# Gated scan and expert layer on one core: the last addition of the output rows as an accumulating DMA, and work at other places

## The chip, the core and the metric

The program runs on one core of a Trainium2 chip. The metric is the device time of one execution in microseconds (us): 694.19 is the median of three runs of the kernel before, which lie between 693.59 and 695.44.

## What is computed

The input x is 8 batches of 1024 tokens of 256 numbers. Two layers follow each other, each with a layer norm ahead of it, one behind it and a residual. The first mixes, for each token, the two best of four gated linear recurrences over the tokens:

```python
gate_logits = einsum('bsd,dm->bsm', x, gate_W)
top_vals, top_idx = top_k(gate_logits, 2);  weights = softmax(top_vals)
g, v, d = (x @ W[m] + b[m] for each mixer m)          # Wg, Wv, Wd
a = 0.001 + 0.998 * sigmoid(d)
h = linear_scan(sigmoid(g) * tanh(v), a)              # h_t = a_t h_{t-1} + x_t
return sum over m of comb[..., m] * h[m]              # comb: weights at top_idx, else 0
```

The second sends each batch row to one of eight experts, by the mean of its normed tokens:

```python
z = layernorm(x) * ln_g + ln_b;  z_bn = batchnorm(mean(z, tokens))
probs = softmax(z_bn @ Wr + br);  idx = argmax(probs);  gate = probs[idx]
h = relu(z @ W_down[idx] + b_down[idx])               # 256 -> 64
return (h @ W_up[idx] + b_up[idx]) * gate             # 64 -> 256
```

Around them: x = x + layernorm(mix(layernorm(x))), then x = x + layernorm(experts(layernorm(x))).

## The kernel before

Each engine has its program written out by hand; the order of its lines is the order of its work, and semaphores tie the engines together. Every engine's program has three parts: `run_first` for batch 0, `run` for batches 1 to 6, which a loop of three turns with two batches each repeats (`iterations`, L230), and `last` for batch 7. In these, `bt` is the batch whose recurrences are computed, `nx` the next one, whose x is loaded, normed, split in two 16-bit halves (`xh`, `xl`) and weighed for the mixers, and `pv` the previous one, whose second layer is done between the products of `bt`.

A batch's recurrences are 8 planes (4 mixers by 2 halves of 128 channels). For each plane TensorE makes 6 products of 128 channels by 512 tokens (gate, decay and value, for two chunks of tokens), 48 in a batch, numbered i=0 to 47. A product is six 16-bit matmuls (L1332) into one of three banks of `ps_main`; ScalarE evacuates each with its sigmoid or tanh (`evacuate`, L550 to L580, into `gate_s`, `decay_s` and `hid`), and TensorE waits for the bank that it wants next. VectorE multiplies (L902), scans (L884) and weighs each plane with `comb_all` (`weigh`, L896), the token weights, which come broadcast through DRAM. GpSimd's accumulating DMAs add up planes of `hid` (`add_plane`, L477). In `last` the batch is cut in two halves of 512 tokens, so that the tail can start on the first.

What is done for `pv` hangs on numbers i in the programs of TensorE (`run`, L1441) and ScalarE (L677), which say ahead of which product or evacuation a step stands. TensorE turns the added planes into token rows (`turn_planes`, L1346); VectorE takes their moments (`a_moments`, L784), adds the residual into `resid`, takes moments again; ScalarE norms (`normalise_t`, L616, into `normed`); TensorE turns the result (`turn_u`), ScalarE copies it to `u_split` (`high_u`, L587); VectorE and TensorE (`route`) make the router's logits, VectorE picks the index (`route_pick`, L942), SyncE reads it and loads that expert's weights (`load_expert`, L328). Then TensorE's `down` (L1382), ScalarE's `hidden_part` and `high_h`, VectorE's `join_h` and `low_h` (L964), TensorE's `up` (L1391), moments and shift, and ScalarE's `scale_rows` (L639), which leaves the normed expert rows in `normed`, or in `x_in` under the name `late_rows` for batches 6 and 7. `normed` also carries x's halves on their way to `xh` and `xl`. GpSimd makes the roots of the variances (`power`, L464).

At a batch's end VectorE's `finish` (L987) adds `normed` to `resid`; for batches 6 and 7 `finish_late` (L994) does it tile by tile. SyncE's `store` (L340) then writes `resid` out at the end of its turn in `run`, after the next x, this batch's x for `resid` (`load_resid`, L335), the expert, x's moved halves (`move_x`) and `comb_all` (`load_weights`, L314).

## Time and profile before

| | |
|---|---|
| median of three runs | 694.19 us (693.59 to 695.44) |
| the profiled execution | 692.3 us |
| its span, first to last instruction | 690.5 us |
| TensorE (PE) busy | 610.8 us, 88% |
| VectorE (DVE) busy | 586.9 us, 85% |
| ScalarE (ACT) busy | 460.5 us, 67% |
| GpSimd (POOL) busy | 100.9 us, 15% |
| granted TensorE clock, mean | 0.958 of full |

The span has a start up to some 31 us, batch 0 up to about 100 us, six batches of the loop with 76.5 us each (177.0 to 253.5 is the second of them), and the last batch with its tail from about 560 us. Busy shares are means over these stages. In the loop TensorE's matmuls follow each other nearly without a break, and what counts there is what it waits for; behind 643 us the engines work one after another and the chain of waits is what counts. Matmuls are pipelined: one is drawn with 0.38 us, but the next starts 0.22 us after it. PEld is TensorE's loading of weights, SPq the queue of DMAs that SyncE issues.

### The profile page before, as it was taken

To read this page: it belongs to the slowest core of one execution; us is meant where nothing else is said; L and a number is where in the kernel's file an instruction comes from. 1 tells how busy PE (TensorE), PEld (TensorE's weight loads), DVE (VectorE), ACT (ScalarE), POOL (GpSimd) and SP (SyncE) were. 2 spreads that over 40 slices of the span, in tenths; PEclk is the share of its full clock that TensorE was granted. 3 is DMA by queue.
4 is the path that set the end of the run, shared out by engine and by line. 5 is a ranking of instruction groups with operands and counts; after the bars stand their busy time and mean duration, and the time that the engine had idled before them with its cause. 6 is when DMAs were issued, how large, how long until landed. Compare 5 with 4: busy or idle time off the path is not lost. (4 is left out here: it accounts for less than half of the span.)

```text
span 690.5 us, 10277 instructions
## 1 busy us (share of the span) xinstructions
PE 610.8 (88%) x3259; PEld 312.7 (45%) x3259; DVE 586.9 (85%) x1096; ACT 460.5 (67%) x789; POOL 100.9 (15%) x103
## 2 busy tenths in 40 slices
PE   3799999899999999899999999899999997989432
PEld 1345454445544554445544554444544554444321
DVE  6699688998889888998889888998889888778846
ACT  3657555896579666986589666987589667657213
POOL 2002012101121102101121102101121101112101
PEclk9999999999999999999999999999999999999655
DMA  8652636162533617171724626161816433301121
GB/s 227 142 183 39 146 63 243 20 130 47 204 103 75 120 59 251 31 133 33 233 73 92 103 79 227 42 122 31 271 33 116 79 122 124 59 14 32 31 72 61
DMA packets 74905, 73.63 MB, mean 107 GB/s; under 512 B 36166, under 2 KB 66154, under 8 KB 74858
## 3 DMA queue, kind: packets, MB, share of 16 engines
q1 hardware_dynamic: 69676, 56.30, 28.8%
q0 software_dynamic: 5184, 16.78, 13.3%
q8 instruction: 22, 0.36, 0.2%
q14 instruction: 23, 0.19, 0.1%
HBM read 38.85 MB, written 8.52 MB: 69 GB/s over the span
## 5 line engine op out<-in xcount | busy, mean ns | idle before, releaser
L1332 PE MATMUL ps_main<-xh,w_hi 128*128 128x512 f16 x768 | 293.9, 383 | 16.0 <-ACT gate_s L574 9.3
L1332 PE MATMUL ps_main<-xh,w_lo 128*128 128x512 f16 x768 | 293.5, 382 | 0.0
L1332 PE MATMUL ps_main<-xl,w_hi 128*128 128x512 f16 x768 | 293.3, 382 | 0.0
L884 DVE TENSOR_TENSOR_SCAN hid<-decay_s,hid 128x1024 f32<-128x1024 f32 (+1 forms) x64 | 138.2, 2159 | 6.6
L574 ACT ACTIVATE decay_s<-ps_main,vecs 128x512 f32<-128x512 f32 x128 | 88.1, 688 | 72.9 <-PE ps_main L1332 72.1
L574 ACT ACTIVATE hid<-ps_main,vecs 128x512 f32<-128x512 f32 x128 | 88.3, 690 | 62.3 <-PE ps_main L1332 61.9
L1332 PEld LDWEIGHTS ps_main<-xh,w_hi 128*128 128x128 f16 x768 | 76.4, 99 | 110.1 <-ACT gate_s L574 16.1
L1332 PEld LDWEIGHTS ps_main<-xl,w_hi 128*128 128x128 f16 x768 | 75.7, 99 | 92.4 <-issue 3.0
L1332 PEld LDWEIGHTS ps_main<-xh,w_lo 128*128 128x128 f16 x768 | 75.7, 99 | 85.0 <-issue 2.3
L574 ACT ACTIVATE gate_s<-ps_main,vecs 128x512 f32<-128x512 f32 x128 | 87.7, 685 | 29.9 <-PE ps_main L1332 28.8
L896 DVE TENSOR_TENSOR hid<-hid,comb_all 128x1024 f32<-128x1024 f32 (+1 forms) x72 | 79.6, 1106 | 2.5
L902 DVE TENSOR_TENSOR hid<-gate_s,hid 128x1024 f32<-128x1024 f32 (+1 forms) x72 | 79.4, 1103 | 1.4 <-ACT hid L574 0.5
L580 ACT ACTIVATE decay_s<-decay_s 128x1024 f32<-128x1024 f32 (+1 forms) x72 | 69.0, 959 | 0.0
L477 POOL DMA_DIRECT2D hid<-hid x36 | 31.8, 882 | 246.5 <-DVE hid L896 238.4
L1283 PE MATMUL ps_aux<-ident,normed 128*128 128x128 f32 x144 | 22.3, 317 | 33.8 <-DVE normed L824 20.5
L464 POOL TENSOR_TENSOR root_a<-root_in_a,neg_half 128x8 f32<-128x8 f32 (+1 forms) x9 | 19.3, 2142 | 136.7 <-DVE root_in_a L792 136.7
L1283 PEld LDWEIGHTS ps_aux<-ident,normed 128*128 128x128 f32 x144 | 19.3, 164 | 38.4 <-ACT normed L616 17.3
L1346 PE MATMUL ps_aux<-ident,hid 128*128 128x128 f32 x256 | 31.2, 280 | 3.0 <-DMA hid<-hid 2.6
L1346 PEld LDWEIGHTS ps_aux<-ident,hid 128*128 128x128 f32 x256 | 29.5, 145 | 5.7 <-issue 3.4
L784 DVE BATCH_NORM_STATS2 stats_a<-ps_aux 128x6 f32<-128x256 f32 x64 | 22.1, 416 | 11.6 <-PE ps_aux L1346 11.6
L616 ACT ACTIVATE normed<-resid,shift_t,root_t 128x256 f32<-128x256 f32 x60 | 30.4, 592 | 2.2 <-DVE shift_t L799 2.2
L784 DVE BATCH_NORM_STATS2 stats_y<-ps_aux 128x6 f32<-128x256 f32 x64 | 22.1, 417 | 11.4 <-PE ps_aux L1392 11.4
(139 smaller groups left out, 581.3 us busy)
## 6 DMA issues: line engine op xcount, KB each, us to landing
comb_all<-comb_dram SPq DMA_DIRECT2D x32, 512.0 KB, 5.5
hid<-hid POOLq DMA_DIRECT2D x28, 512.0 KB, 4.6
x_in<-in_L_attn_x SPq DMA_DIRECT2D x16, 512.0 KB, 10.0
resid<-in_L_attn_x SPq DMA_DIRECT2D x8, 1024.0 KB, 5.9
out<-resid SPq DMA_DIRECT2D x7, 1024.0 KB, 9.9
hid<-hid POOLq DMA_DIRECT2D x8, 256.0 KB, 3.3
expert<-experts SPq DMA_DIRECT2D x8, 192.5 KB, 2.2
w_stage<-in_L_attn_Wg SPq DMA_DIRECT2D x4, 256.0 KB, 3.5
```

The costliest lines, as they stand in the source:

```text
L464: pool.tensor_tensor(root[key][:, span(c)], root_in[key][:, span(c)], neg_half[:, span(c)], ALU.pow).then_inc(rooted, units(c))
L477: pool.dma_start(hid[:, p + KT, tokens(c)], hid[:, p, tokens(c)], accum_op=ALU.add).then_inc(plane_added[p], 16)
L574: act.activation(dst, ps_main[:, i % BANKS], ACT.Tanh if kind == VALUE else ACT.Sigmoid, bias=vecs[:, col:col + 1], scale=Q_W).then_inc(ma ...
L580: act.activation(d, d, ACT.Copy, bias=0.001, scale=0.998).then_inc(decay_ready, 1)
L616: ins = act.activation(out[:, t], rows[:, t], ACT.Identity, bias=shift[key][:, t:t + 1], scale=root[key][:, t:t + 1])
L784: ins = dve.bn_stats(out=stats[key][:, t], in_=rows(t))
L884: dve.tensor_tensor_scan(states(pc), staged(decay_s, pc, pc.c), states(pc), start, ALU.mult, ALU.add).then_inc(scanned, 1)
L896: dve.tensor_tensor(src, src, comb_all[:, m, tokens(pc.c)], ALU.mult).then_inc(weighed, 1)
L902: dve.tensor_tensor(v, staged(gate_s, pc, pc.c), v, ALU.mult).then_inc(input_ready, 1)
L1283: ins = pe.transpose(ps_aux[:, KT * cc + k, tile(t % (T // C))], normed[:, t, k * P:(k + 1) * P], ident[:])
L1332: ins = pe.matmul(ps_main[:, i % BANKS], w[:, 3 * m + kind, k, half * P:(half + 1) * P], v[:, bt.par, span(c), k], start=(n == 0), stop=(n ...
L1346: ins = pe.matmul(ps_tok[:, t, k * P:(k + 1) * P], hid[:, p, tile(t)], ident[:], is_transpose=True, start=(p == TURNED[0] and t % 2 == 0), ...
```

## The change

- `finish` and VectorE's addition for batches 0 to 6 are gone. GpSimd's `add_rows` waits until ScalarE's normed expert rows are written (`y_normed`) and issues one DMA that adds 1 MB of `normed` (for batch 6 `late_rows`) to `resid`; `rows_added` tells when it has landed. In `run` it is GpSimd's last step; in `last` it stands behind the roots of t.
- `store` waits for `rows_added` and stands one turn later: in `run` straight behind the load of the next x and ahead of `load_resid`. SyncE's program has no loop any more; its eight turns are written out. In `last` the store of batch 5 comes first, and that of batch 6 stands ahead of `load_expert(bt)`.
- ScalarE waits for `rows_added` before it overwrites `normed` (`normalise_t`) and `late_rows`.
- In `run` TensorE turns the planes at i=3 (was 4), does `down` at 30 (29), `up` at 38 (40), the next batch's gates at 41 (40). ScalarE makes both halves of u at i=20 (were 20 and 21), `high_h` at 33 and 35 (31 and 34), `shares` at 47 (44), the first rows at 44 (45). VectorE's `x_moments`, `scale_x` and `weights_of` stand a plane or a part of one later.
- In batch 0 VectorE's preparations of the weights are in another order, TensorE makes the first gates and turns the weights at i=4 (6 and 8), the next gates at 38 (36). In the last batch `up` is at i=32 (29), and at the end VectorE makes the moments of both halves before the shifts.

The diff, cut to its core, by engines. SyncE and GpSimd:

```diff
@@ -336,7 +337,7 @@
                              ).then_inc(resid_loaded, 16)
 
             def store(pv):
-                sp.wait_ge(out_ready, done(pv))
+                sp.wait_ge(rows_added, 16 * pv.n + 16)
                 sp.dma_start(out_t[bass.ds(pv.n, 1)].rearrange("a p t d -> p (a t) d"), resid[:, pv.par]
                              ).then_inc(out_stored, 16)
 
@@ -417,26 +418,32 @@
                 load_resid(bt)
                 load_weights(bt, nx)
 
-            def run(bt, nx, pv):
+            def run(bt, nx, pv, before):
                 load_next_x(bt, nx)
+                if before:
+                    store(before)
                 load_resid(bt)
                 load_expert(pv)
                 move_x(nx)
                 load_weights(bt, nx)
-                store(pv)
-
-            def last(bt, pv):
+
+            def last(bt, pv, before):
+                store(before)
                 load_resid(bt)
                 load_expert(pv)
+                store(pv)
                 load_expert(bt)
-                store(pv)
                 for part in range(2 * C):
-                    sp.wait_ge(out_ready, C * bt.n + part + 1)
+                    sp.wait_ge(out_ready, part + 1)
                     s = slice(part * T // (2 * C), (part + 1) * T // (2 * C))
                     sp.dma_start(out_t[bt.n, :, s], t_rows(bt)[:, s]).then_inc(out_stored, 16)
                 sp.wait_ge(out_stored, 16 * (B + 2 * C) + 1)
 
-            iterations(sp, run_first, run, last)
+            turns = [Batch(n, n % 2, n == B - 1) for n in range(B)]
+            run_first(turns[0], turns[1])
+            for n in range(1, B - 1):
+                run(turns[n], turns[n + 1], turns[n - 1], turns[n - 2] if n > 1 else None)
+            last(turns[B - 1], turns[B - 2], turns[B - 3])
 
 
         @block.gpsimd
@@ -477,6 +484,12 @@
                 pool.dma_start(hid[:, p + KT, tokens(c)], hid[:, p, tokens(c)], accum_op=ALU.add
                                ).then_inc(plane_added[p], 16)
 
+            def add_rows(pv, rows):
+
+                pool.wait_ge(y_normed, T * (pv.n + 1) + 1)
+                pool.sem_inc(rows_go, 1)
+                pool.dma_start(resid[:, pv.par], rows[:], accum_op=ALU.add).then_inc(rows_added, 16)
+
...
                 add_plane(bt, 3)
                 power("y", y_root_in, y_root, pv)
+                add_rows(pv, normed)
...
                 power("t", t_root_in, t_root, bt, 1)
+                add_rows(pv, late_rows)
                 power("y", y_root_in, y_root, bt, 0)
                 power("y", y_root_in, y_root, bt, 1)
```

ScalarE, the waits and `run`:

```diff
             def normalise_t(pv, ts):
 
                 act.wait_ge(t_scaled, done(pv))
+                act.wait_ge(rows_added, 16 * pv.n)
                 normalise("t", t_rows(pv), ts, u_ready, C if ts[-1] == T - 1 else 0)
...
             def scale_late_rows(bt, c):
                 act.wait_ge(y_scaled, B + c)
+                act.wait_ge(rows_added, 16 * (B - 1))
                 scale_rows(bt, tiles(c), late_rows)
...
                         normalise_t(pv, tiles(1))
                     if i == 20:
                         high_u(pv, 0)
-                    if i == 21:
                         high_u(pv, 1)
                     if i == 24:
...
                         hidden_part(pv, 1)
-                    if i == 31:
+                    if i == 33:
                         high_h(pv, 0)
-                    if i == 34:
+                    if i == 35:
                         high_h(pv, 1)
                     if i == 44:
-                        shares(nx)
-                    if i == 45:
                         act.wait_ge(xh_moved, 16 * nx.n)
                         act.wait_ge(xl_moved, 16 * nx.n)
                         act.wait_ge(y_scaled, pv.n + 1)
                         scale_rows(pv, (0, 1, 2), normed)
+                    if i == 47:
+                        shares(nx)
                     evacuate(bt, i, bank, False)
```

VectorE: `finish` and `finish_late`, the start of `run_first`, the end of `last`:

```diff
-            def finish(pv):
-
-                dve.wait_ge(y_normed, T * (pv.n + 1) + 1)
-                rows = t_rows(pv)
-                dve.tensor_tensor(rows, normed[:], rows, ALU.add).then_inc(out_ready, C)
-
             def finish_late(b, c):
 
                 rows = t_rows(b)
                 for t in tiles(c):
                     dve.wait_ge(y_normed, T * b.n + t + 2)
                     ins = dve.tensor_tensor(rows[:, t], late_rows[:, t], rows[:, t], ALU.add)
-                    if b.cut and t % 2:
+                    if t % 2:
                         ins.then_inc(out_ready, 1)
-                if not b.cut:
-                    ins.then_inc(out_ready, C)
...
             def run_first(bt, nx):
                 prep = linker(prep_link, 0)
                 pcs = pieces(bt)
+                prepare_router(prep)
                 mixer_low(1)
                 prepare_down(prep, 0)
-                set_ones()
                 rank_mixers(bt)
                 weights_of(bt)
-                mixer_low(2)
+                set_ones()
+                prepare_down(prep, 1)
                 copy_weights(bt, True)
-                mixer_low(3)
-                prepare_router(prep)
-                prepare_down(prep, 1)
                 prepare_up_biases(prep)
...
                 weigh(bt, pcs[15])
+                low_u(bt, 0)
                 a_moments(bt, 1)
-                low_u(bt, 0)
                 residual(bt, 1)
                 t_moments(bt, 1)
                 scale_t(bt, 1)
                 normalise("t", t_rows(bt), t_scaled, u_ready, bt, 1)
                 route_logits(bt)
-                finish_late(pv, None)
+                route_pick(bt)
                 low_u(bt, 1)
                 join_h(bt, 0)
-                route_pick(bt)
                 join_h(bt, 1)
                 low_h(bt, 0)
                 low_h(bt, 1)
                 y_moments(bt, 0)
+                y_moments(bt, 1)
                 scale_y(bt, 0)
-                y_moments(bt, 1)
+                scale_y(bt, 1)
                 finish_late(bt, 0)
-                scale_y(bt, 1)
                 finish_late(bt, 1)
```

TensorE: `run_first`, `run` and `last`:

```diff
                 for i, bank in enumerate(banks(bt)):
                     if i == 0:
                         turn_vecs()
-                    if i == 2:
                         turn_x(bt, 1)
-                    if i == 6:
+                    if i == 4:
                         first_gates(bt)
-                    if i == 8:
                         turn_weights(bt)
-                    if i == 21:
+                    if i == 20:
                         hidden_bias()
-                    if i == 36:
+                    if i == 38:
                         pe.wait_ge(experts_ready, 6)
                         gates(nx)
                     product(bt, i, bank, True)
...
             def run(bt, nx, pv):
                 for i, bank in enumerate(banks(bt)):
-                    if i == 4:
+                    if i == 3:
                         turn_planes(pv, (4, 5, 6, 7))
                     if i == 22:
                         turn_u(pv)
                     if i == 26:
                         route(pv)
-                    if i == 29:
+                    if i == 30:
                         down(pv)
-                    if i == 40:
+                    if i == 38:
                         up(pv)
+                    if i == 41:
                         gates(nx)
...
                         turn_u(pv)
-                    if i == 16:
+                    if i == 17:
                         route(pv)
-                    if i == 23:
+                    if i == 24:
                         down(pv)
-                    if i == 29:
+                    if i == 32:
                         up(pv)
-                    if i == 39:
+                    if i == 38:
                         pe.wait_ge(y_normed, T * (B - 2) + T // C + 1)
                         turn_planes(bt, TURNED, 0)
-                    if i == 47:
-                        turn_u(bt, 0)
                     product(bt, i, bank, False)
+                turn_u(bt, 0)
                 pe.wait_ge(y_normed, T * (B - 1) + 1)
                 turn_planes(bt, TURNED, 1)
```

The order of the instructions on SyncE at the program's end shows where the store of batch 6 stands against the two loads of an expert's weights. Before (`load_resid`, `load_expert` for batches 6 and 7, the store, the four parts of batch 7):

```order
L335 DMA resid<-in_L_attn_x 128x8x256
L327 TENSOR_LOAD index
L327 ISA x2
L328 ISA
L328 DMA expert<-experts 128x385
L327 TENSOR_LOAD index
L327 ISA x2
L328 ISA
L328 DMA expert<-experts 128x385
L340 DMA out<-resid 128x8x256
L436 DMA out<-resid 128x2x256 x4
```

After, with the same steps:

```order
L336 DMA resid<-in_L_attn_x 128x8x256
L328 TENSOR_LOAD index
L328 ISA x2
L329 ISA
L329 DMA expert<-experts 128x385
L341 DMA out<-resid 128x8x256
L328 TENSOR_LOAD index
L328 ISA x2
L329 ISA
L329 DMA expert<-experts 128x385
L439 DMA out<-resid 128x2x256 x4
```

The store, the first DMA into `out`, was behind both loads of `expert` and now stands between them.

On ScalarE around i=19 to 21 in the loop, `normed` x8 is `normalise_t`, `u_split` are `high_u`'s copies, and `gate_s`, `decay_s` and `hid` are evacuations. Before:

```order
L574 ACTIVATE decay_s<-ps_main,vecs 128x512
L586 ISA
L587 ACTIVATE u_split,u_sums<-ps_aux 128x512
L586 REGISTER_ALU
L587 ACTIVATE u_split,u_sums<-ps_aux 128x512
L573 REGISTER_ALU
L574 ACTIVATE hid<-ps_main,vecs 128x512
L586 REGISTER_ALU
L587 ACTIVATE u_split,u_sums<-ps_aux 128x512
L586 REGISTER_ALU
L587 ACTIVATE u_split,u_sums<-ps_aux 128x512
```

After:

```order
L589 ACTIVATE decay_s<-ps_main,vecs 128x512
L601 ISA
L602 ACTIVATE u_split,u_sums<-ps_aux 128x512
L601 REGISTER_ALU
L602 ACTIVATE u_split,u_sums<-ps_aux 128x512
L601 REGISTER_ALU
L602 ACTIVATE u_split,u_sums<-ps_aux 128x512
L601 REGISTER_ALU
L602 ACTIVATE u_split,u_sums<-ps_aux 128x512
L588 REGISTER_ALU
L589 ACTIVATE hid<-ps_main,vecs 128x512
```

All four copies of u now stand ahead of the evacuation into `hid` (i=20), where two of them came behind it.

On GpSimd at the program's end the rows are the additions of planes (`hid`), the roots of a, t and y, and in the new program the addition into `resid`. Before:

```order
L477 DMA hid<-hid 128x512
L464 TENSOR_TENSOR root_t<-root_in_t,neg_half 128x4
L477 DMA hid<-hid 128x512 x2
L464 TENSOR_TENSOR root_a<-root_in_a,neg_half 128x4
L464 TENSOR_TENSOR root_t<-root_in_t,neg_half 128x4
L464 TENSOR_TENSOR root_y<-root_in_y,neg_half 128x4 x2
```

After:

```order
L484 DMA hid<-hid 128x512
L471 TENSOR_TENSOR root_t<-root_in_t,neg_half 128x4
L484 DMA hid<-hid 128x512 x2
L471 TENSOR_TENSOR root_a<-root_in_a,neg_half 128x4
L471 TENSOR_TENSOR root_t<-root_in_t,neg_half 128x4
L491 DMA resid<-x_in 128x2048
L471 TENSOR_TENSOR root_y<-root_in_y,neg_half 128x4 x2
```

The addition for batch 6 comes behind the last roots of a and t and ahead of those of y.

## Rows read from the trace of the kernel before

**Rows 1.** Windows table, a loop batch: busy us (x instructions) per engine, clock, DMA, GB/s
```profile
177.00:253.50 76.50, 72.72 (x400) 36.92 (x398) 68.62 (x122) 56.84 (x97) 11.84 (x8) 1.00 0.44 114
```

**Rows 2.** Waits of TensorE, whole span: waiter <- releaser: us, times, longest
```profile
PE ps_main L1332 <- ACT gate_s L574: 9.3, 10, 1.2
PE ps_aux L1391 <- DVE up_in L964: 5.7, 2, 2.9
...
PE ps_aux L1382 <- DMA expert<-experts: 3.1, 6, 0.8
...
PE ps_misc L1303 <- DMA xl<-normed: 1.3, 1, 1.3
```

**Rows 3.** Timeline of TensorE: start us, duration us, what, [idle before <-releaser]
```profile
31.46 0.39 PE L1332 MATMUL ps_main<-xh,w_hi 128*128 128x512 f16 x1 [3.66 <-ACT decay_s L574]
...
175.55 0.39 PE L1332 MATMUL ps_main<-xh,w_hi 128*128 128x512 f16 x1 [0.58 <-ACT gate_s L574]
...
213.73 0.38 PE L1332 MATMUL ps_main<-xl,w_hi 128*128 128x512 f16 x1
215.22 0.39 PE L1332 MATMUL ps_main<-xh,w_hi 128*128 128x512 f16 x1 [1.10 <-ACT gate_s L574]
215.44 0.38 PE L1332 MATMUL ps_main<-xh,w_lo 128*128 128x512 f16 x1
...
218.45 1.90 PE L1382 MATMUL ps_aux<-u_split,expert 128*128 128x512 f16 x8 [0.47 <-DMA expert<-experts]
```

**Rows 4.** Timeline of ScalarE, second batch of the loop
```profile
207.28 0.60 ACT L587 ACTIVATE u_split<-ps_aux 128x512 f16<-128x512 f32 x1
...
214.28 0.21 ACT L592 ACTIVATE r<-r 128x8 f32<-128x8 f32 x1 [1.10 <-DVE r L938]
```

**Rows 5.** Timeline of VectorE, same batch
```profile
176.72 2.27 DVE L987 TENSOR_TENSOR resid<-normed,resid 128x2048 f32<-128x2048 f32 x1
180.55 2.75 DVE L784 BATCH_NORM_STATS2 stats_a<-ps_aux 128x6 f32<-128x256 f32 x8 [1.55 <-PE ps_aux L1346]
...
187.82 1.22 DVE L896 TENSOR_TENSOR hid<-hid,comb_all 128x1024 f32<-128x1024 f32 x1
```

**Rows 6.** The page's DMA issues: queue, count, KB each, median us to landing
```profile
comb_all<-comb_dram SPq DMA_DIRECT2D x32, 512.0 KB, 5.5
hid<-hid POOLq DMA_DIRECT2D x28, 512.0 KB, 4.6
x_in<-in_L_attn_x SPq DMA_DIRECT2D x16, 512.0 KB, 10.0
...
out<-resid SPq DMA_DIRECT2D x7, 1024.0 KB, 9.9
hid<-hid POOLq DMA_DIRECT2D x8, 256.0 KB, 3.3
expert<-experts SPq DMA_DIRECT2D x8, 192.5 KB, 2.2
```

**Rows 7.** SyncE's queue, timeline; last, the DMA issues after 600 us
```profile
178.34 2.58 SPq L314 DMA_DIRECT2D comb_all<-comb_dram  x4
...
667.00 0.49 SPq L328 DMA_DIRECT2D expert<-experts  x1
...
out<-resid SPq DMA_DIRECT2D x1, 1024.0 KB, 4.5
```

**Rows 8.** The chain of work that ended last: start us, us, what
```profile
657.72 1.02 POOL root_t L464
...
666.10 0.05 DVE index L942
...
666.17 2.76 DVE resid L994 x8
...
670.28 1.88 PE ps_aux L1382 x4
```

**Rows 9.** Timeline of ScalarE at the end
```profile
685.49 1.93 ACT L639 ACTIVATE x_in<-ps_aux,shift_y,root_y 128x256 f32<-128x256 f32 x4 [1.82 <-DVE shift_y L980]
```

69 lines of the change are left out of this document (30 added, 39 removed).

## The prediction

> **What bounds the kernel now.** I read the windows table first. In a batch of the loop TensorE shows 72.7 us of 76.5 and VectorE 68.6 [rows 1]; what is left of TensorE's time are short stalls, and a gain in the loop must come out of them. The waits of TensorE name them [rows 2], and its timeline places them [rows 3]. Three kinds recur, and I call the 48 products of a batch i=0 to 47. First, ten waits on ScalarE's evacuation of `gate_s`, 9.3 us: four of 0.58 at i=3 (the row at 175.55; batches 2, 4, 5, 6), the other six, some 1.1 each, at i=27 (the row at 215.22). Second, `down` waits for the expert's weights in each of six batches, 3.1 us together. Third, outside the steady part, 1.3 us for the moved halves of x in batch 0, and `up` in the last batch. A matmul starts 0.22 after its predecessor but is drawn 0.38 long [rows 3], so a stall costs 0.17 more in starts than its idle: 215.22 lies 1.49 after 213.73, 1.27 too late. Behind the loop the chain of waits reads as one thread, with VectorE's eight additions of the previous rows, 2.76 us, standing in it [rows 8].
>
> **The change, part by part.** All prices are against the profiled execution, 692.3 us (span 690.5 and 1.8 around it), which is 1.9 under the median of 694.2 of the runs shown; I add that at the end.
>
> *VectorE's addition goes in the loop.* Six instructions of 2.27 [rows 5] leave VectorE, 13.6 us busy. I price that at 0: straight behind it VectorE sat 1.55 us waiting for TensorE's turned planes [rows 5], so it would only wait longer. What it is worth must show through the next edit.
>
> *The planes are turned at i=3, not 4* (D). The four stalls at i=3 come since ScalarE first scales five tiles and then evacuates bank 0. With the turning there, TensorE has work just when it would stand still: 4 x (0.58 + 0.17) = **-3.0**. The bound on the other side is 0, if the planes' own inputs aren't there yet.
>
> *VectorE's lead and the router* (C). The turned planes come one product, 6 x 0.22 = 1.3 us, earlier in TensorE's order, and with them the chain to the router's logits. ScalarE stood 1.10 us for these logits before evacuating bank 24 [rows 4], and that is what TensorE waits for at i=27. Not all comes back: the logits also need TensorE's `route`, which isn't earlier, so about half, 0.8 of the 1.3 in starts at best. Against it, ScalarE now makes both halves of u at i=20 in a row: bank 20 is evacuated two copies, 1.1 us [rows 4], later. TensorE has turned u in the meantime and has a product of 1.3 in hand, so I take 0.3 of that. Net -0.5, six times: **-3.0**. Bounds: -6.6 if the 1.10 goes whole, +2.1 if VectorE gains no lead and 0.35 a batch is lost.
>
> *`down` one product later* (B). `down` waited 0.47 in the row at 218.45, 0.5 on the mean [rows 2, 3]; a product of 1.3 ahead of it covers that: 6 x (0.52 + 0.17) = **-4.1**, bound 0.
>
> *New waits* (F). The sigmoid of the shares moves from i=44 to 47, just ahead of the product of `comb` and `share` that TensorE turns at the batch's end, and `high_h` moves from 31 and 34 to 33 and 35, closer to `up`, which itself moves from 40 to 38. Each has less than a product of room. No row shows such a wait; the bounds are 0 and the largest wait of this sort, 1.2 a place [rows 2], of which 0.2 in each of six batches is nearest to the 0 that these edges show now: **+1.2**, range 0 to 2.4.
>
> *The addition as a DMA, in the loop.* It runs from `normed` on GpSimd's queue at the batch's end. Accumulating 256 KB takes 3.3 us and 512 KB 4.6 [rows 6], so 1 MB some 7.2. Who waits: ScalarE at i=19 before it overwrites `normed`, over 20 us later; SyncE's store, which now stands behind the loads of x; behind it the load of `resid`, which is used a batch later, and the expert's, 30 us on. GpSimd's next instruction, the root of a, comes only after the planes. Price 0; the cover is those distances. The store itself moves only from the end of one turn past the two loads of the next. Writing SyncE's turns out: 0, its queue waits for data nearly all the time.
>
> The Trainium skill (DMA: Bandwidth & Descriptors, Anatomy of one DMA — SWDGE (gpsimd) path) prices a transfer on this path at 2.0 us plus bytes over 436 GB/s, an estimate of 3.2 us for the 512 KB. The rows show 4.6, so the trace disagrees, and I leave it at that; by the page 1 MB would need 4.4 and the end (E, below) would come up to 2.8 us sooner.
>
> *Batch 0* (A). Gates of the next batch move from i=36 to 38, past the 1.3 us wait: -1.5. Against it, the first weights are turned at i=4 straight behind the gates. TensorE now stands idle 3.66 before i=7 [rows 3]; there it will stand with three products, 3.9 us, fewer done, while the ranking, with fewer copies ahead of it on VectorE, ends some 2.7 sooner: +1.2. **-0.3**, bounds -1.5 and +2.5.
>
> *Last batch and end* (E). `up` moves from i=29 to 32, so three products fill a wait of up to 2.9 [rows 2]; VectorE, which goes on from there without pause, gets perhaps 1.1 of it: -1.1. Then the chain: the 2.76 of additions leave VectorE's path between the index and `down`. What is late next is the expert's load. It was asked for at 667.00, 0.8 after the index, and takes 2.2 [rows 6, 7], so 669.2 would allow `down` at 669.3 and not 670.28. But SyncE now first waits for the addition to store batch 6. GpSimd asks for that after the root of t, which ends at 658.74 [rows 8]: with 0.5 for the issue it lands at 658.7 + 0.5 + 7.2 = 666.4, the store takes 4.5 [rows 7], 670.9, and the expert's load stands behind it in the same queue; x, asked for straight behind a store, takes 10.0 beside the store's 9.9 [rows 6]. With 0.5 for its own bytes, 671.4: +1.1 against 670.28. At the end VectorE makes both halves' moments before the first shift; ScalarE's gap of 1.82 [rows 9] closes while its first tiles start some 1.0 later: -0.8. Together **-0.8**, bounds -3.9 (the expert not held up) and +2.0 (the addition takes twice 4.6).
>
> **Sum:** -3.0 - 3.0 - 4.1 + 1.2 - 0.3 - 0.8 = -10.0; 692.3 - 10.0 = 682.3, and with 1.9 for the median 684.2.
>
> **The rivals.** *1. VectorE's lead is eaten* before the logits, by a later load or since ScalarE itself is full between i=19 and 33. For it: ScalarE waits only for VectorE there, and the recovered time must pass through it. Against: three banks of buffer. C is +2.1 instead of -3.0: 684.2 + 5.1 = 689.3.
>
> *2. Slower: the addition delays `comb_all`.* The 1 MB starts just before the four loads of `comb_all`, on the same 16 DMA engines. VectorE wants the first at 187.82; it was asked for at 178.34 and takes 5.5 [rows 5 to 7]: 4.0 to spare, 2.7 with a lead of 1.3. If the load gets nothing until the addition is done, it is up to 7.2 late: VectorE stands 4.5, hence 3.2 behind its old place, and ScalarE and TensorE wait that much more at i=27: C becomes 6 x 3.2 = +19.2, and 684.2 + 22.2 = 706.4. The kernel ends slower than 694.2 once C is over +7.0, 1.2 a batch, which is a delay of 2.7 + 1.3 + 1.2 = 5.2. Against it: the delay must be most of the addition's length, though the loads are asked for after the addition has begun.
>
> The Trainium skill (DMA: Bandwidth & Descriptors, Queues, rings and completion order) says an engine takes turns between queues packet by packet; by that the load would lose about half of the time, 3.6 us, and rival 2 would not come about. No run here shows the two side by side.
>
> *3. The change doesn't reach the steady part:* ScalarE, not TensorE, paces i=19 to 33, B and C both vanish: 684.2 + 7.1 = 691.3, hardly told from no change. For it: each of these waits lies where ScalarE runs without pause; against it: after i=33 ScalarE waits for TensorE again, so time that TensorE saves there is kept.
>
> **How the numbers follow.** Forecast 0.56; rival 1 0.20; rival 3 0.14; rival 2 0.10. A measurement tells 0.3%, 2.1 us, from no change: faster is under 692.1. The forecast and rival 1 are, and a third of rival 3 with its spread: 0.80; same 0.11; slower 0.09. The range leaves out rival 2 and the far half of rival 3: from 680.0 (C and E a little better) to 691.5.
>
> **What would show it.** In the new trace: no additions of 2.27 on VectorE; i=3 without a wait before it; ScalarE's wait for the logits under 0.7, not 1.1; `down` without a wait for the expert in the loop, and with one at the end, where the store is asked for before the expert; the 1 MB landing after 7 us. I am wrong if a batch stays at 76 us, if VectorE waits for `comb_all`, or if batch 0 ends later by more than 2.

## The result, and the profile after

The changed kernel takes 699.89 us (median of four runs, 698.94 to 700.43), the kernel before beside it 693.89: a ratio of 1.0093 with a 95% interval of 1.0051 to 1.0135. It is slower by 0.9%, where 1.4% faster was forecast. Its profiled execution took 700.2 us with a span of 698.0, against 692.3 and 690.5.

From the page of the changed kernel, span, and busy time of each engine:

```profile
span 698.0 us, 10188 instructions
...
PE 618.4 (89%) x3259; PEld 312.5 (45%) x3259; DVE 571.4 (82%) x1082; ACT 460.8 (66%) x789; POOL 100.8 (14%) x110
```

VectorE is busy 15.5 us less, as it should be without the additions of seven batches (13.6 and 2.8 us, [rows 5, 8]). TensorE, ScalarE and GpSimd have the work that they had; TensorE's drawn time grows by 7.6. The two traces, cut where the first product (i=0) of each batch starts, tell where the 7.5 us of span come from:

| us | start | batch 0 | 1 | 2 | 3 | 4 | 5 | 6 | 7 and tail |
|---|---|---|---|---|---|---|---|---|---|
| before | 14.2 | 80.0 | 76.7 | 77.9 | 75.9 | 76.5 | 76.7 | 76.5 | 136.1 |
| after | 16.6 | 80.5 | 75.7 | 79.9 | 77.3 | 79.6 | 77.4 | 76.1 | 135.0 |
| difference | +2.4 | +0.4 | -1.0 | +2.0 | +1.4 | +3.1 | +0.7 | -0.4 | -1.1 |

A batch that no turn of the loop touches (1 and 6) is shorter, as forecast, though by 0.4 to 1.0 and not by some 1.5. Batches 2 to 5 are longer, by 7.2 together, and the loop's two turns back lie at the ends of batches 2 and 4. The waits of TensorE after (what waits and releaser; us in total, times, longest) show the same place, beside [rows 2]:

```profile
PE ps_main L1327 <- issue: 7.4, 2, 3.8
PE ps_aux L1377 <- DMA expert<-experts: 5.6, 1, 5.6
...
PE ps_main L1327 <- ACT gate_s L589: 3.6, 7, 0.9
PE ps_aux L1386 <- DVE up_in L969: 3.5, 2, 2.9
...
PE ps_main L1327 <- ACT hid L589: 2.9, 6, 0.5
```

The ten waits on `gate_s`, 9.3 us, are seven of 3.6 now, and the expert's weights are waited for once, at the end, and no more in the loop. New are two waits of 3.7 on the mean with "issue" behind them: TensorE waited there for nothing that a semaphore shows. TensorE's timeline at the first turn, after:

```profile
248.31 0.38 PE L1327 MATMUL ps_main<-xl,w_hi 128*128 128x512 f16 x1
248.58 0.28 PE L1306 MATMUL ps_misc<-ident,comb 128*32 128x128 f32 x1
252.66 0.60 PE L1327 MATMUL ps_main<-xh,w_hi 128*128 128x512 f16 x1 [3.80 <-issue]
253.05 0.63 PE L1327 MATMUL ps_main<-xh,w_lo 128*128 128x512 f16 x1
```

L1306 turns `comb`, the next batch's token weights, the last work of a batch; the next row is the first product of batch 3. Between their starts lie 4.08 us. In the kernel before, they lie 1.43 apart at this turn and 0.11 at the second (3.86 after):

```profile
247.34 0.27 PE L1311 MATMUL ps_misc<-ident,comb 128*32 128x128 f32 x1
248.77 0.39 PE L1332 MATMUL ps_main<-xh,w_hi 128*128 128x512 f16 x1 [1.16 <-ACT hid L574]
```

What TensorE does in between stands in the view of one line, the loop's own: its three branches in the changed kernel, shortest, middle and longest in ns, then the first and last start (the shortest is the last, which falls through; PEldq stands for TensorE's sequencer, which issues its work):

```profile
L237 PEldq COMPARE_BRANCH  x3: 83/3400/3617, 248.7 to 562.8; - x3
```

and the same for the kernel before:

```profile
L236 PEldq COMPARE_BRANCH  x3: 76/236/3772, 244.6 to 551.5; - x3
```

TensorE's branch back to the loop's head is drawn 3.4 to 3.8 us long in both programs, but for one of 0.24 in the kernel before. The kernel before starts it at 244.6, 2.7 us ahead of the turning of `comb` (247.34), and the matmuls that are queued cover most of it; the changed kernel starts it at 248.7, after the turning (248.58), and nothing covers it. For 3.4 us, the stall's end and the first products, TensorE ran at the lower of its two clocks: the windows table (busy time of each engine, then granted clock, share of the DMA engines, GB/s)

```profile
252.40:255.80 3.40, 3.14 (x8) 1.19 (x9) 2.08 (x3) 0.60 (x2) 0.92 (x1) 0.50 0.41 84
```

gives 0.50 of 2.4 GHz. Its matmuls are 0.43 us apart there and not 0.22, which costs 1.6 us more at each of the two turns. Behind the stall of 1.43 of the kernel before, the clock stayed at 1.00. Stalls and clock together: 2.65 + 1.55 at the first turn, 3.75 + 1.6 at the second, 9.6 us. Without them the changed span would be 2 us under the one before.

The weights that TensorE turns last came late. VectorE makes `comb` (`weights_of`) behind plane 6 and not ahead of it, and ScalarE its share at i=47 and not 44. VectorE's timeline has the last step of `comb` after, and before:

```profile
248.31 0.21 DVE L872 TENSOR_TENSOR comb<-share,chosen 128x32 f32<-128x32 f32 x1
243.20 0.22 DVE L867 TENSOR_TENSOR comb<-share,chosen 128x32 f32<-128x32 f32 x1 [0.34 <-ACT share L548]
```

It ends at 248.52 after, 0.14 us ahead of the branch, and at 243.42 before, 1.2 ahead of it. TensorE's sequencer, which in the kernel before had reached the branch 2.7 us ahead of the matmuls, now stands in front of the wait for `comb`, and reaches the branch only behind it.

### The profile page after: what moved, and what is told of

It reads as the page before. It is cut to its first block and busy times, and to the rows that moved or that the text cites. A ratio compares the mean times of both kernels' runs of the same rounds, so it can differ in the third digit from the quotient of the medians.

```text
span 698.0 us, 10188 instructions
## 1 busy us (share of the span) xinstructions
PE 618.4 (89%) x3259; PEld 312.5 (45%) x3259; DVE 571.4 (82%) x1082; ACT 460.8 (66%) x789; POOL 100.8 (14%) x110
## 5 line engine op out<-in xcount | busy, mean ns | idle before, releaser
L1327 PEld LDWEIGHTS ps_main<-xl,w_hi 128*128 128x128 f16 x768 | 76.1, 99 | 93.7 <-issue 5.2
L901 DVE TENSOR_TENSOR hid<-hid,comb_all 128x1024 f32<-128x1024 f32 (+1 forms) x72 | 79.6, 1106 | 3.0 <-DMA comb_all<-comb_dram 0.5
L602 ACT ACTIVATE u_split<-ps_aux 128x512 f16<-128x512 f32 x32 | 18.7, 594 | 20.5 <-PE ps_aux L1278 20.5
L471 POOL TENSOR_TENSOR root_x<-root_in_x,neg_half 128x8 f32<-128x8 f32 (+1 forms) x9 | 18.8, 2086 | 92.3 <-DVE root_in_x L797 92.3
```

What stands on the lines that cost most here:

```text
L471: pool.tensor_tensor(root[key][:, span(c)], root_in[key][:, span(c)], neg_half[:, span(c)], ALU.pow).then_inc(rooted, units(c))
L901: dve.tensor_tensor(src, src, comb_all[:, m, tokens(pc.c)], ALU.mult).then_inc(weighed, 1)
L1327: ins = pe.matmul(ps_main[:, i % BANKS], w[:, 3 * m + kind, k, half * P:(half + 1) * P], v[:, bt.par, span(c), k], start=(n == 0), stop=(n ...
```

## The experiments

All ratios are to runs of the kernel before on the same chip, with 95% intervals. "Without a loop" is TensorE's program written out, with no branch.

### The turn back to the loop's head

**a_early**, the changed kernel with the weights early:

```diff
                     if i == 44:
+                        shares(nx)
                         act.wait_ge(xh_moved, 16 * nx.n)
...
-                    if i == 47:
-                        shares(nx)
...
                 scale_y(pv)
+                weights_of(nx)
                 multiply(bt, pcs[6])
                 scan(bt, pcs[6])
                 weigh(bt, pcs[6])
-                weights_of(nx)
```

> The changed kernel with one thing of its loop put back: ScalarE makes the shares at i=44 again and VectorE the token weights ahead of the products of plane 6, so that the product of comb and share which TensorE turns at a batch's end is ready early. In the changed kernel TensorE stands 4.1 and 3.9 us at the two turns back to the loop's head (its branch is drawn 3.6 and 3.4 us long and starts only when the turned weights are out), and the granted clock falls to half for 3.4 us behind each, where the kernel before lost 1.2 us and nothing. Theory: the late weights hold the branch, and its time then stands in the open. Then the first stall falls to about 1.2 us, the second to 0 to 1.2, no fall of the clock follows, and the time falls from 699.9 by 6 to 9.5 us, to 690.5 to 694. Rival: the 1 MB of the addition, which moves at the same moment, holds up the loading of TensorE's code: then both stalls stay at 3 us or more and the time stays within 2 us of 699.9.

Measured: 693.45 us, 1.0008 (0.9975 to 1.0040): 6.4 less than 699.89, level with the kernel before. The branch starts 2.0 us ahead of the turning of `comb`; from there to the next product it is 1.93 and 2.26 us (4.08 and 3.86 in the changed kernel), and no fall of the clock follows. The direction is the theory's; the stalls are longer than the 1.2 that I had expected, and the second is no shorter than the first. This trace has one more loss, away from the turns: in batch 4, 81.1 us long, VectorE waits 2.18 us for `comb_all`, TensorE then 2.19 before i=27, and the clock falls behind that for 3.4 us:

```profile
371.44 0.39 PE L1326 MATMUL ps_main<-xh,w_hi 128*128 128x512 f16 x1 [2.19 <-ACT gate_s L589]
```

**b_late**, the kernel before with `weights_of(nx)` moved behind `weigh(bt, pcs[6])`, and nothing else:

> The kernel before, with VectorE's token weights of the next batch moved behind the weighing of plane 6, as the changed kernel has them; nothing else. There is no addition by DMA at the batch's end. Theory of the late weights: TensorE's branch starts up to 3 us later, its stall at the first turn back to the loop's head grows from 1.2 us to 3 or more and a fall of the clock comes with it; at the second turn, where the kernel before had a branch of 0.24 us, either 3 us as well or nothing. Time 697 to 703. Rival, the addition's traffic: 692 to 695, branches as in the kernel before.

Measured: 703.27 us, 1.0165 (1.0121 to 1.0208), just above the expected range and ten us slower by one moved line, with no addition by DMA anywhere. TensorE's timeline at its first turn:

```profile
246.18 0.28 PE L1311 MATMUL ps_misc<-ident,comb 128*32 128x128 f32 x1 [0.33 <-DVE comb L867]
250.36 0.60 PE L1332 MATMUL ps_main<-xh,w_hi 128*128 128x512 f16 x1 [3.89 <-issue]
```

and its branches, in the view of the loop's line:

```profile
L236 PEldq COMPARE_BRANCH  x3: 83/3600/3704, 246.3 to 564.5; - x3
```

The wait for `comb` itself is 0.33 us. The branch starts at 246.3, behind the turning at 246.18, and 3.89 us of idle follow. The clock falls behind both turns, for 6.8 and 3.4 us.

**a_peflat**, the changed kernel without a loop on TensorE:

```diff
-            iterations(pe, run_first, run, last)
+            turns = [Batch(n, n % 2, n == B - 1) for n in range(B)]
+            run_first(turns[0], turns[1])
+            for n in range(1, B - 1):
+                run(turns[n], turns[n + 1], turns[n - 1])
+            last(turns[B - 1], turns[B - 2])
```

> The changed kernel with TensorE's program written out, its eight batches one behind the other with no loop and no branch; all other engines as they are. Theory: what TensorE loses at the two turns is the branch, so both stalls and both falls of the clock go and the time falls by 8 to 10 us, to 690 to 692. If TensorE waits there for something else (the moved halves of x, the weights themselves), stalls of 3 us stay in the same places and the time stays near 699.9.

Measured: 687.34 us, 0.9913 (0.9882 to 0.9945). The weights are as late as before, and the place where 4 us were lost reads

```profile
246.99 0.38 PE L1327 MATMUL ps_main<-xl,w_hi 128*128 128x512 f16 x1
247.26 0.28 PE L1306 MATMUL ps_misc<-ident,comb 128*32 128x128 f32 x1
247.38 0.38 PE L1327 MATMUL ps_main<-xh,w_hi 128*128 128x512 f16 x1
```

0.12 us from the turning to the next product. 12.5 us less than with the loop is more than was expected, and more than the 9.6 of the trace. Between the two traces, batches 2 to 5 are 9.2 us shorter; most of what is beyond that lies in batch 0 (2.3), whose length varies from trace to trace.

**b_peflat**, the kernel before without a loop on TensorE:

> The kernel before with TensorE's program written out, no loop and no branch on TensorE. If the two branches cost the kernel before what its profiled execution shows, 1.2 us at the first and nothing at the second, the time is 691.5 to 693. If that execution was lucky at the second turn (its branch took 0.24 us there, those of the other traces 3.4 to 3.8), it is 688 to 691. The changed kernel with TensorE written out took 687.3: what is left between the two is the worth of the rest of the change, forecast at 10.0 us less without the late weights.

Measured: 693.28 us, 0.9989 (0.9971 to 1.0008). The branch costs the kernel before 0.7 us, which its own scatter hides, though its stalls at the two turns are 1.3 us longer in the trace of before and 3.9 in that of b_again than without a branch. Part of it comes back: behind the stalls of 1.39 us and more in these two traces the wait at i=3 is missing, some 0.8 us each. Without a loop the rest of the change is worth 0.9913 against 0.9989, 0.8% or 5.3 us, where ten were forecast.

**p_early**, the changed kernel with both edits, early weights and no loop:

> The changed kernel with TensorE written out and with the shares and the token weights made early (both edits at once). Theory: without a branch the late weights cost only the 0.27 us by which TensorE's last product of a batch waits for them, six times: 1.6 us, so 685 to 686.5, against 687.3 with late weights; against 6.5 us with the branch. Rival: the late weights cost 5 us or more by themselves: 682 or less.

Measured: 686.74 us, 0.9878 (0.9838 to 0.9917). Against 687.34 the early weights are worth 0.6 us, or 2.4 by the ratios, whose intervals overlap: a small thing without a branch, 6.4 us with one.

What was then open is why 693.5 with early weights and the loop stands 6 us over this. Three runs more:

**a_early45**, early weights as in a_early, and ScalarE's rows back from i=44 to 45:

```diff
                     if i == 44:
                         shares(nx)
+                    if i == 45:
                         act.wait_ge(xh_moved, 16 * nx.n)
```

> The changed kernel with early weights and, besides, ScalarE's first three expert rows at i=45 and not 44, both as before. Theory: the rows at i=44 hold the evacuation of bank 44, for which TensorE's last product, and behind it the branch, is kept waiting; with them at 45 the branch starts 2.7 us ahead of the end of the queued work, the stalls at the two turns are 1.1 to 1.4 us instead of 1.8 and 2.2, and the time is 1 to 3 us under the 693.5 of early weights alone: 690.5 to 692.5. Rival: the rest of the branch's price is its length alone: 693 to 694.5.

Measured: 689.64 us, 0.9936 (0.9907 to 0.9964), 4 us under a_early, 0.9 under the expected range, and faster than the kernel before with the loop in place. Its branches:

```profile
L237 PEldq COMPARE_BRANCH  x3: 83/3601/4673, 243.4 to 550.4; - x3
```

and TensorE's timeline at the second turn:

```profile
400.37 0.27 PE L1306 MATMUL ps_misc<-ident,comb 128*32 128x128 f32 x1
401.61 0.39 PE L1327 MATMUL ps_main<-xh,w_hi 128*128 128x512 f16 x1 [0.97 <-ACT hid L589]
```

The second branch starts 2.7 us ahead of the turning, not 2.0, and takes 3.6: 1.24 us to the next product, near the 1.43 of the kernel before at its first turn. The first starts 2.6 ahead, but is drawn 4.7 us and leaves 2.48. The theory holds for the start of the branch; its length varies by itself. The 4 us are not shown to come from there: the way from the turning to the next product is 3.7 us at both turns together and 4.2 in a_early. Batch 4, where a_early lost its 2.19 us and the clock, is 3.4 us shorter here, 1.0 of it at the turn; TensorE's wait is there too, 1.05 us, without a fall of the clock.

**b_late_flat**, the kernel before with late weights and without a loop:

> The kernel before with late token weights (703.3 with its loop) and TensorE written out. Theory: late weights cost only through the branch; without it TensorE's last product of a batch waits 0.5 to 0.6 us for them (less what the stall at i=3 gives back), so 692.5 to 696. If the weights' delay costs by itself, it stays at 700 or more.

Measured: 694.24 us, 0.9999 (0.9976 to 1.0021). TensorE waits 0.34 us for the weights and goes straight on:

```profile
248.44 0.28 PE L1311 MATMUL ps_misc<-ident,comb 128*32 128x128 f32 x1 [0.34 <-DVE comb L867]
248.56 0.38 PE L1332 MATMUL ps_main<-xh,w_hi 128*128 128x512 f16 x1
```

So the four cells on the kernel before are: early weights, 1 with the loop and 0.9989 without; late weights, 1.0165 with it and 0.9999 without. Neither costs anything alone; together they cost 1.65%.

**b_again**, the kernel before once more:

> The kernel before once more, unchanged, for a second trace of its two branches. If the branch of 0.24 us at the second turn is its rule: again under 0.5 us there, and no stall. If it was one execution's: 3.4 to 4.7 us as in the other traces, with a stall of 1 to 2.4 us behind it.

Measured: 694.89 us in one run. Its branches:

```profile
L236 PEldq COMPARE_BRANCH  x3: 83/3743/4968, 246.3 to 554.9; - x3
```

3.7 us at the second turn, not 0.24: the short one of the profiled execution before is not the program's rule. From the turning to the next product it is 2.77 and 1.39 us. Of the 16 taken branches in eight traces with a loop, 15 took 3.4 to 5.0 us.

### The addition alone

**b_rows**, the kernel before with the addition as a DMA (`add_rows`, `store`, SyncE's turns, the two waits of ScalarE), and all other orders as they were:

> The kernel before with the addition as an accumulating DMA, the store a turn later and SyncE written out, as the changed kernel has them; every other order as before. Theory: VectorE only waits longer for the turned planes in the loop, the cover of 20 us and more holds for the DMA, and at the end 2.8 us of additions go against an expert load that stands behind a store: 691 to 694.5. Rival, the addition holds up comb_all, the planes or TensorE's code: over 696, with VectorE waiting for comb_all or stalls of TensorE over 2 us at the two turns.

Measured: 693.2 us, 0.9988 (0.9962 to 1.0015). The part that names the change does nothing to the time that these runs resolve. VectorE waits for `comb_all` once in this trace, 0.2 us.

### Batch 0

**a_first**, the changed kernel with the start and batch 0 of the kernel before (VectorE's order there, ScalarE's and TensorE's `run_first`):

> The changed kernel with its start and batch 0 as they were before: the order of VectorE's preparations, and ScalarE's and TensorE's steps of batch 0, TensorE's second half of x turned at i=2 and not ahead of all products. Theory: the 2.8 us by which batch 1 begins later (97.1 against 94.3) come from these orders, 2.4 of them from the first product (16.6 against 14.2): the time falls by 2 to 3.5 us, to 696.4 to 698. Rival: the later start is given back by work that waits anyway in batch 0: within 1 us of 699.9.

**p_first**, the same without a loop on TensorE:

> The changed kernel with TensorE written out and with the start and batch 0 as they were before (both edits at once; TensorE's written-out program alone gave 687.3). Theory: the first product starts 2.4 us sooner and batch 1 some 2.8 us, and with no branch behind it this is kept: 683.5 to 685.5. Rival: the first batch's planes or another wait gives it back, as in the run with the old start and the loop: 686.5 to 688.5.

Measured: 700.0 us, 1.0103 (1.0072 to 1.0133), and 690.09, 0.9937 (0.9908 to 0.9966), against 1.0093 and 0.9913 with the new orders: nothing won, and the second is above both ranges named for it. In the traces the first product starts at 14.6 and 15.0 instead of 16.6 and 17.4, but batch 1 is 77.5 and 77.4 us long and not 75.7: TensorE, turning the planes at i=3, now waits for the last one, which VectorE weighs later (TensorE's timeline of a_first in batch 1):

```profile
100.77 0.44 PE L1342 MATMUL ps_aux<-ident,hid 128*128 128x128 f32 x2 [1.53 <-DVE hid L902]
```

So the later start is given back in batch 1. How much of the rest is batch 0 can't be told: its length alone lies between 76.3 and 81.4 us in the traces of the two kinds of order.

### The terms of the loop

Four kernels on p_early (early weights, no loop), one edit each. Single runs of one kernel lie up to 8.6 us apart here, so I read the length of an undisturbed batch (4 and 6) in the traces: 75.94 and 75.93 us in p_early.

**p_u**, ScalarE's second half of u back at i=21:

> The changed kernel with TensorE written out and early weights (together 686.7), and ScalarE's second half of u back at i=21. In the changed kernel TensorE waits 0.65 us before i=23 for bank 20, which is evacuated behind four copies of u, and 0.7 before i=27 for ScalarE, which waits for the router's logits; between i=24 and 33 ScalarE runs without a pause. Theory: ScalarE and the logits pace this stretch, so the wait before i=23 goes, the one before i=27 grows by as much, and a batch stays at 75.9 us: 685.7 to 687.7. Rival: the wait for bank 20 is a loss of its own: 3.9 us less, 682 to 684.

Measured: 687.55 us, 0.9924 (0.9896 to 0.9952); a batch 75.43 and 75.43. The time lies where the theory put it, but in the trace the wait for bank 20 goes, and the one before i=27 grows by 0.14 only. By the trace alone the rival holds: 0.5 us a batch are lost by the four copies in a row.

**p_dn**, `down`, `up`, the gates and `high_h` back at 29, 40, 40, 31 and 34:

> TensorE written out and early weights, and down, up, the gates and the two steps of ScalarE on h back at 29, 40, 40, 31 and 34 as before. Theory that ScalarE paces i=24 to 33: down waits 0.6 us for the expert's weights again, but the 0.42 us of small waits before i=31 to 33 go, so a batch is 0 to 0.25 longer: 686.7 to 688.2. By the forecast's term for down each batch is 0.69 longer: 690.8.

Measured: 688.79 us, 0.9943 (0.9924 to 0.9962); 0.6 above the range of the theory; a batch 75.93 and 75.93, the same. `down` waits for the expert again, but from i=31 to 33 TensorE waits that much less: moving `down` by itself is worth nothing.

**p_pl4**, the planes turned at i=4:

> TensorE written out and early weights, and the planes turned at i=4 again. The forecast's term for this step: TensorE stands 0.63 to 0.75 us before i=3 in nearly every batch, 3.8 to 4.5 us: 690 to 691.5. Rival: the stall is made up by i=33, where ScalarE paces: 686 to 688.

Measured: 689.53 us, 0.9948 (0.9923 to 0.9972), between the two ranges; a batch 76.56 and 76.56, 0.62 more. The wait before i=3 is back:

```profile
174.70 0.38 PE L1326 MATMUL ps_main<-xh,w_hi 128*128 128x512 f16 x1 [0.68 <-ACT gate_s L589]
```

**p_rows**, ScalarE's split of x at i=34 and 35, VectorE's part behind `low_h`:

```diff
                         normalise_x(nx, tiles(1))
-                        high_rows_x(nx, 0)
-                        high_rows_x(nx, 1)
...
+                    if i == 34:
+                        high_rows_x(nx, 0)
                     if i == 35:
                         high_h(pv, 1)
+                        high_rows_x(nx, 1)
```

> TensorE written out and early weights, and ScalarE's split of the next x (2.0 us, at i=27) moved to i=34 and 35, with VectorE's part of it behind low_h. Theory that ScalarE paces i=24 to 33: with 2.0 us less for it there, the small waits before i=31 to 33, 0.42 us a batch, go: 683 to 685; unless the moved halves of x then come late for the gates at i=41, which would show as a wait there. Rival: ScalarE does not pace it: the same as without, 686 to 688.

Measured: 704.21 us, 1.0153 (1.0072 to 1.0235). The 0.42 us of small waits before i=31 to 33 go, as by the theory that ScalarE paces these; but the moved halves come too late for the gates:

```profile
244.58 0.17 PE L1298 MATMUL ps_misc<-gw,xh 128*128 128x8 f16 x1 [2.11 <-DMA xl<-normed]
```

and such a wait stands in each of the six batches, 13.4 us in all; behind three of them the clock falls. The time is far outside both ranges, and nothing is won. The step had 2 us too little cover at its new place.

### Together

**best**, p_early with the second half of u at i=21 and the last expert's load ahead of the store of batch 6:

> The changed kernel with TensorE written out, early weights, ScalarE's second half of u at i=21, and the last expert's load ahead of the store of batch 6. Sum of the parts: 686.7 with the first two; the wait for bank 20 goes, 0.5 us a batch by its trace, 3.0; the load takes 2.2 us instead of 3.6, 1.4 at most: 682 to 685.5. If the load is not what down waits for, 683.5 to 686.5.

Measured: 684.67 us, 0.9874 (0.9845 to 0.9903), span 681.7: faster than both kernels, by 1.3% and 2.2%. At the end, the load's size and time from issue to landing:

```profile
expert<-experts SPq DMA_DIRECT2D x1, 192.5 KB, 2.3
```

and in the changed kernel, where the load stands behind the store:

```profile
expert<-experts SPq DMA_DIRECT2D x1, 192.5 KB, 3.6
```

`down` starts 1.3 us sooner after `route`.

## Why the prediction was wrong

Forecast -10.0 us, measured +7.5 in the traces. By its terms, where the loop's are the differences between the two traces in the starts of TensorE's products of batches 1 to 6, at the places that are named:

| term | forecast | shown |
|---|---|---|
| D, planes at i=3 | -3.0 | -3.1 |
| C, lead and u | -3.0 | -0.4 (-4.3 before i=27, +3.9 before i=23) |
| B, `down` later | -4.1 | -1.7 (i=28 to 33) |
| F, new waits | +1.2 | +11.0, of which 9.6 by the branch and the clock behind it |
| A, batch 0 | -0.3 | +2.8 at batch 1's start |
| E, last batch and end | -0.8 | -1.1 |

The last column sums to the 7.5. Of the 17.5 us between forecast and trace the branch is 9.6, and it turns the sign; A, C and B, each some 2.4 to 3.1 short of its price, are the rest. Without the branch the change would still not have won ten: by these traces it would have been 2 us, and between the two programs without a loop it was 5.3.

**The step that failed is F.** I saw that the shares moved to i=47, "just ahead of the product of `comb` and `share` that TensorE turns at the batch's end", bounded the wait by 1.2 us a place and took 0.2. The wait for the weights is within that: the six ends of a batch are each 0.06 to 0.3 us longer by it, 1.2 together, and an undisturbed batch of a_peflat, with late weights, is no longer than one of p_early. What I left out is what stands behind that wait in TensorE's own program: a branch, at two of the six ends. I had asked for each wait who waits for it, but only of instructions that the page counts as busy, and a branch isn't. The trace of before had it, 3.77 us at 244.62 under a stall of 1.16 whose named releaser is ScalarE (in the timeline of before, with the result). The bound of 1.2 for an unknown wait was taken from waits of another sort.

The Trainium skill (Runtime: NRT & Kernel Launch, Instruction fetch mechanics) says that a taken branch whose target isn't in the loaded window waits until the target is fetched by DMA. The trace agrees: in the changed kernel's window from 248 to 254 us two instruction packets of 16 KB move and nothing else (GB/s in 40 slices of the window, then the packets, then the queue's),

```profile
GB/s 0 0 0 0 0 0 0 0 0 0 0 109 0 0 0 0 0 0 0 0 0 0 0 0 0 0 0 0 0 0 0 0 0 0 0 0 0 109 0 0
DMA packets 2, 0.03 MB, mean 5 GB/s; under 512 B 0, under 2 KB 0, under 8 KB 0
...
q8 instruction: 2, 0.03, 2.2%
```

one in the stall at 249.7, one behind it at 253.6. It also rules out that the addition's traffic held up the code. Around the branch of before that took 0.24 us, from 398 to 402.5, no packet moves at all:

```profile
DMA packets 0, 0.00 MB, mean 0 GB/s; under 512 B 0, under 2 KB 0, under 8 KB 0
```

Nor does an instruction packet of 16 KB move in the whole pass of the loop behind it, from 382.0 to 549.9 us, where the other passes have one every 31 us or less. Why the code was at hand there, and not in the second trace of the same kernel, no run shows.

**C** had two halves. The lead came nearly as forecast, -4.3 us for -4.8: ScalarE's wait for the logits is 0.70 and not 1.10 [rows 4], TensorE's wait before i=27 0.57 and not 1.10 [rows 3]. The price of the four copies of u was put at 0.3 us since TensorE had "a product of 1.3 in hand"; it is the whole 0.65 in starts, 0.5 of it idle, since bank 20 is the one that i=23 wants. ScalarE's rows of after (start, duration; the wait in brackets):

```profile
209.10 0.70 ACT L589 ACTIVATE hid<-ps_main,vecs 128x512 f32<-128x512 f32 x1
...
215.66 0.21 ACT L607 ACTIVATE r<-r 128x8 f32<-128x8 f32 x1 [0.70 <-DVE r L943]
```

and TensorE's products that wait for them:

```profile
209.86 0.39 PE L1327 MATMUL ps_main<-xh,w_hi 128*128 128x512 f16 x1 [0.49 <-ACT hid L589]
...
216.60 0.39 PE L1327 MATMUL ps_main<-xh,w_hi 128*128 128x512 f16 x1 [0.57 <-ACT gate_s L589]
```

**B**: the wait for the expert went, but TensorE, which arrives 0.6 sooner, then waits 0.42 in each batch at i=31 to 33 for the banks that ScalarE evacuates without a pause. That is the third rival's mechanism, at 31 to 33; p_rows shows it by taking ScalarE's work away, and p_dn that `down` at its old place is as good. C's lead it did not take.

**D** came out as priced. **A**: the gates' 1.5 came (1.45 less from i=34 to 47 of batch 0), but I left out that the second half of x is turned ahead of all products (i=2 to 0), which puts the first product at 16.6 and not 14.2, 2.4 us. The new order of VectorE spares batch 1 the wait of 1.5 that a_first has.

**E**: right in mechanism, and in size since its misses cancel. To the index the last batch is 1.25 us shorter (1.1 forecast), from `down` to the end 0.3 (0.8 forecast). The addition landed 7.0 us after its issue (7.2 forecast), the store was issued 1.3 us ahead of the expert's load, which took 3.6 us and not 2.2, and `down` waited for it, 0.4 later behind the index than before (4.57 and 4.18 us); 1.1 was forecast.

**The addition in the loop**: price 0, and b_rows measured 0, but with less cover than the forecast saw. VectorE's saved time became waiting for the planes (timeline of after, where [rows 5] had 1.55), and `comb_all` was waited for once:

```profile
180.50 2.75 DVE L789 BATCH_NORM_STATS2 stats_a<-ps_aux 128x6 f32<-128x256 f32 x8 [2.09 <-PE ps_aux L1341]
...
189.22 1.22 DVE L901 TENSOR_TENSOR hid<-hid,comb_all 128x1024 f32<-128x1024 f32 x1 [0.50 <-DMA comb_all<-comb_dram]
```

The forecast compared the addition with the loads of `comb_all` and left out the 16 KB that save the token weights, for which these loads wait. GpSimd's addition and SyncE's save and loads after, then save and loads before:

```profile
177.12 0.92 POOL L491 DMA_DIRECT2D resid<-normed  x1 [10.57 <-ACT normed L655]
178.44 0.35 SPq L321 DMA_DIRECT2D comb_dram<-comb_rows  x1
185.26 2.07 SPq L315 DMA_DIRECT2D comb_all<-comb_dram  x4
...
176.82 0.36 SPq L320 DMA_DIRECT2D comb_dram<-comb_rows  x1
178.34 2.58 SPq L314 DMA_DIRECT2D comb_all<-comb_dram  x4
```

The save, issued 1.3 us behind the addition, lands after 6.8 us and not 1.4, so the loads start 5.3 us later against the save, and the 4.0 to spare are gone.

**Rival 2** named 706 us and the right sign, which was luck: the loss is the branch's. Its mechanism is there, but small: in the kept traces with the addition VectorE waits for `comb_all` 0.2 to 3.3 us in all, in the five without it never. In the changed kernel it was 0.5 us in one place, where 5.2 a batch would have been needed.

## What to carry to other kernels

Ask of a wait that is moved to the end of a loop's body what the sequencer does next: a branch that starts late stands in the open with its full length, since only the work queued ahead of it covers it. Look for that in the rows of the loop's own line and at idle time put down to "issue", since a branch is in no busy time; keep the last waits of a body early, or write the engine's program out. And a wait that is taken away in a stretch where another engine runs without pause comes back a few products later: read the row of that engine before the gain is counted. Where a large transfer is given cover, follow also the small transfers beside it for which others wait.

## What the hardware showed

- TensorE's taken branch was drawn 3.4 to 5.0 us long, 15 times of 16; those of the other engines at the same line took 0.04 to 0.06.
- Behind a stall of about 4 us the granted clock was 0.50 for 3.4 us or 6.8; behind stalls of 1.2 to 2.8 us at a turn it mostly stayed at 1.00, though it fell behind one of 2.46 (b_rows). Away from the turns it fell behind the 2.19 us of a_early and behind three of the six waits of 2.1 to 2.6 us in p_rows.
- Beside the 1 MB addition a small transfer suffers more than the large ones: the 16 KB that save the token weights land after 5.9 us (median) and not 1.4 (in batch 1, which has no addition ahead of it, after 1.4 in this kernel too), while the 512 KB loads of `comb_all` stay at 5.5. The rows of after, from issue to landing:

```profile
comb_all<-comb_dram SPq DMA_DIRECT2D x32, 512.0 KB, 5.5
...
resid<-normed POOLq DMA_DIRECT2D x6, 1024.0 KB, 7.5
...
comb_dram<-comb_rows SPq DMA_DIRECT2D x8, 16.0 KB, 5.9
```
